# One pick signal per portion of four, and gathers in pairs behind TensorE's blocks

## The reference, cut to what matters

```python
# 32 tables; ids: [1024, 32]; 64 numbers for each field of each row
e = jnp.stack([tbl_f[ids[:, f]] for f in range(32)], axis=1)        # [1024, 32, 64]
p, q = e[:, ROW_IDX], e[:, COL_IDX]                                 # the 496 pairs i < j
z = jnp.einsum('bne,hne,bnh->bn', p, kernel, q)                     # [1024, 496]
h = jnp.concatenate([z, dense_ctx], axis=1)                         # 496 + 16 = 512
h = jnp.maximum(h @ W_top1 + b_top1, 0.0)                           # 512
h = jnp.maximum(h @ W_top2 + b_top2, 0.0)                           # 256
y = h @ W_top3                                                      # [1024, 1]
```

## Time and profile before

| | |
|---|---|
| median of 3 runs | 469.64 us (468.99 to 469.80) |
| the profiled execution, its own time | 470.17 us |
| its span, first to last instruction | 468.4 us |
| PE busy (matmuls) | 412.4 us, 88% |
| DVE busy | 353.3 us, 75% |
| ACT busy | 337.2 us, 72% |
| POOL busy | 242.3 us, 52% |
| mean granted TensorE clock | 0.967 |

### The profile page before, as it was taken

The page is one execution under the profiler, slowest core; times in us unless marked ns, Lnnn a source line. Parts: engine busy times, 40 slices in busy tenths (PEclk is TensorE's granted clock), DMA queues, the critical chain, the costliest instruction groups (busy, mean ns, idle before and its releaser), DMA issues.

```text
span 468.4 us, 13663 instructions
## 1 busy us (share of the span) xinstructions
PE 412.4 (88%) x4890; PEld 307.4 (66%) x4890; DVE 353.3 (75%) x449; ACT 337.2 (72%) x2889; POOL 242.3 (52%) x260
## 2 busy tenths in 40 slices
PE   6655779788989998999989998999989998999997
PEld 6544565667757775767757765767757775667775
DVE  0236767577887978887887978887887978889982
ACT  1125856549887797949797788949797797949992
POOL 5555554555655555565555555565555555552000
PEclk9779879799999999999999999999999999999999
DMA  3456550001111011111111010111111010010000
GB/s 73 152 194 198 187 165 21 18 18 23 24 22 23 20 25 21 24 21 22 21 22 22 20 25 18 23 23 23 23 22 23 20 24 22 22 21 13 2 4 0
DMA packets 14563, 19.27 MB, mean 41 GB/s; under 512 B 7192, under 2 KB 7840, under 8 KB 14496
## 3 DMA queue, kind: packets, MB, share of 16 engines
q0 software_dynamic: 8192, 8.40, 8.3%
q1 hardware_dynamic: 6304, 10.00, 6.6%
HBM read 18.39 MB, written 0.00 MB: 39 GB/s over the span
## 4 chain that ended last, share of the span: by engine, by line
PE 54%; DVE 27%; issue 10%; another core or an unknown queue 5%; DMA 2%; POOL 1%; ACT 0%; DVEq 0%
PE u_ps L633 23%; PE u_ps L626 16%; DVE prod_t L525 12%; DVE prod_s L542 11%; PE side_ps L647 7%; DVE h L556 4%; PE side_ps L682 2%; PE u_ps L609 2%; POOL emb L388 1%; DMA emb<-tbl,ids_sb 1%; PE acc_ps L682 1%; PE side_ps L706 1%; PE u_ps L713 1%; DVE emb_t L514 0%
## 5 line engine op out<-in xcount | busy, mean ns | idle before, releaser
L437 ACT ACTIVATE prod_s<-prod_s 128x64 f32<-128x64 f32 x1405 | 310.9, 297 | 86.6 <-DVE prod_s L542 65.0
L388 POOL DMA_INDIRECT emb<-tbl,ids_sb x256 | 242.1, 946 | 184.2 <-issue 44.0
L437 ACT ACTIVATION_READ_ACCUMULATOR prod_s<-prod_s 128x1 f32 x1405 | 268.8, 225 | 3.3 <-issue 3.2
L525 DVE TENSOR_TENSOR prod_t<-u_ps,emb_t 128x1024 f32<-128x1024 f32 x128 | 154.7, 1219 | 61.9 <-remote 26.0
L626 PEld LDWEIGHTS u_ps<-emb_t,k_sb 64*128 64x128 f32 x2048 | 141.4, 194 | 53.5 <-issue 25.8
L626 PE MATMUL u_ps<-emb_t,k_sb 64*128 64x128 f32 x2048 | 154.1, 286 | 23.3 <-DVE prod_t L525 9.5
L542 DVE TENSOR_TENSOR prod_s<-u_ps,emb 128x1024 f32<-128x1024 f32 (+4 forms) x224 | 150.4, 719 | 21.2 <-PE u_ps L633 11.5
L633 PE MATMUL u_ps<-k_sb,emb_t 64*128 64x512 f32 (+5 forms) x704 | 144.0, 496 | 17.3 <-DVE prod_s L542 10.3
L633 PEld LDWEIGHTS u_ps<-k_sb,emb_t 64*128 64x128 f32 x704 | 62.0, 194 | 48.6 <-DVE prod_s L542 18.5
L647 PE MATMUL side_ps<-prod_t,pick_sb 128*32 128x256 f32 x1024 | 64.2, 382 | 0.2 <-issue 0.2
L682 PE MATMUL acc_ps<-h_t,w_sb 64*128 64x128 f32 x336 | 47.4, 278 | 0.5
(11 more groups left out here) (32 smaller groups left out, 50.9 us busy)
## 6 DMA issues: line engine op xcount, KB each, us to landing
k_sb<-k_pairs SPq DMA_DIRECT2D x9, 512.0 KB, 3.8
emb<-tbl,ids_sb POOLq DMA_INDIRECT x256
k_sb<-k_pairs SPq DMA_DIRECT2D x6, 480.0 KB, 4.4
w_sb<-w SPq DMA_DIRECT2D x1, 1024.0 KB
w_sb<-w SPq DMA_DIRECT2D x1, 512.0 KB
k_sb<-k_pairs SPq DMA_DIRECT2D x1, 448.0 KB
h<-dense SPq DMA_DIRECT2D x8, 8.0 KB
out<-y_row SPq DMA_DIRECT2D x8, 0.5 KB
```

Source lines behind the costliest of these rows:

```text
L388: nc.gpsimd.indirect_dma_start(emb[t % EMBS][:, f * EMBED:(f + 1) * EMBED], None, tables[f], bass.IndirectOffsetOnAxis(ap=ids_sb[:, t, f:f ...
L437: done = nc.scalar.activation(slot, slot, ACT.Copy, accum_out=to[:, column:column + 1])
L525: done = nc.vector.tensor_tensor(prod_t[at % TRING][:].rearrange("p (h x) -> p h x", h=HALVES), u, low.unsqueeze(1).to_broadcast([P, HALVE ...
```

## The change

Only the last matmul of a portion of four picks still counts `picked` up: 4 times per tile instead of 16. The waits of ACT go by portions. The list entries that named single picks are replaced by blocks, so that pairs of gathers wait for one block. In `GATHER_AT` (with gather numbers): 13 from pick 0 and 14 from pick 3 to block 23; 17 from pick 4 and 18 from pick 7 to block 27; 22 from pick 10 to block 31 (where 21 waits already). In `OWN_GATHER_AT`: 26 from pick 15 of the tile before to block 4. In `SECOND_GATHERS`: 15 from pick 1 to block 25, and 18 from pick 5 to block 27.

```diff
 GATHER_AT = [
     ("u", 9), ("u", 10), ("u", 12), ("mlp", 2), ("u", 13), ("u", 14), ("u", 15), ("u", 17), ("u", 18), ("mlp", 4),
-    ("u", 19), ("u", 21), ("u", 22), ("pick", 0), ("pick", 3), ("u", 24), ("u", 26), ("pick", 4), ("pick", 7),
-    ("u", 28), ("u", 29), ("u", 31), ("pick", 10)]
+    ("u", 19), ("u", 21), ("u", 22), ("u", 23), ("u", 23), ("u", 24), ("u", 26), ("u", 27), ("u", 27), ("u", 28),
+    ("u", 29), ("u", 31), ("u", 31)]
 OWN_GATHER_AT = [
-    ("u", 0), ("u", 1), ("u", 3), ("pick", 15), ("u", 4), ("u", 5), ("u", 6), ("u", 8), ("mlp", 0)]
+    ("u", 0), ("u", 1), ("u", 3), ("u", 4), ("u", 4), ("u", 5), ("u", 6), ("u", 8), ("mlp", 0)]
...
 SECOND_GATHERS = [
     ("u", 12), ("u", 13), ("u", 14), ("u", 15), ("turn", 5), ("u", 16), ("u", 17), ("u", 18), ("u", 19), ("u", 20),
-    ("turn", 6), ("u", 21), ("u", 22), ("u", 24), ("u", 25), ("pick", 1), ("u", 26), ("u", 27), ("pick", 5),
+    ("turn", 6), ("u", 21), ("u", 22), ("u", 24), ("u", 25), ("u", 25), ("u", 26), ("u", 27), ("u", 27),
     ("u", 28), ("u", 29), ("u", 30), ("u", 31)]
...
-PORTION = NT // 4
+PORTIONS = 4
+PORTION = NT // PORTIONS
...
-                        if kind == "pick":
-                            pool.wait_ge(picked, at + 1)
-                        else:
-                            pool.wait_ge(slot_emptied, SLOT_USE[kind, 0, at] + 1)
+                        pool.wait_ge(slot_emptied, SLOT_USE[kind, 0, at] + 1)
...
-                        elif kind == "pick":
-                            of = tile - 1 if at >= 3 * PORTION else tile
-                            pool.wait_ge(picked, of * NT + at + 1)
...
-                    act.wait_ge(picked, (t + 1) * NT + PORTION)
+                    act.wait_ge(picked, (t + 1) * PORTIONS + 1)
...
-            act.wait_ge(picked, TILES * NT)
+            act.wait_ge(picked, TILES * PORTIONS)
...
                                 start=(b == 0), stop=(b == NT - 1))
+                if stop % PORTION == 0:
                     done.then_inc(picked, 1)
```

## The result

The changed kernel is slower: 476.61 us, median of 4 runs (476.51 to 476.70), against 469.72 for the kernel before on the same chip (4 runs, 468.99 to 469.98). The ratio is 1.0155 (95% interval 1.0139 to 1.0170), or +6.9 us. The forecast was 465.6 with a range from 459.5 to 475.

What follows compares the result with a forecast made beforehand. It took POOL's gathers holding PE's signals, together with PE, as the bound; 6 x (-1.2 - 0.2 + 0.15) + 7 x 0.5 = -4.0 us gave 465.6 against the median of 469.64, range 459.5 to 475.

Steps and rivals of the forecast that it cites:

- The reading: PE's signals are held while POOL processes gathers, about 1.48 us per gather in a train (a run without a pause).
- I take 1.2: Gather 22 to block 31: DVE's 1.75 us stall before block 2 shrinks, gaining 1.2 us per tile in six tiles.
- nothing changes: Rival: each gather holds as long as before and waits only move; within 0.9 us of 469.6; chance 0.17.
- I take -0.2 per tile: Gathers 17 and 18 to block 27: block 29 reaches DVE at 249.6 instead of 249.80, -0.2 us per tile.
- +0.15 for 13 and 14: Gathers 13 and 14 to block 23: PE's block 27 needs block 24's slot, costing 0.15 us per tile.
- cover gone: Worse case for 13 and 14: DVE's idle 0.52 and 0.54 no longer covers late block 24, costing 0.5 us.
- -0.69 to +0.6: Bounds for 17 and 18 per tile: all of PE's early-turn stop comes back, or the late copy shifts everything.
- some 26 records behind a held signal: Where PE was read to stop before the change: at the early turn (0.27 and 0.42 us) and third block (0.70).
- Gather 26: Moved to block 4: a train of three delays DVE's copy of transposed part 1, +0.5 us in each of seven tiles.
- The late spread takes it back: Rival: the train from gather 25 delays transposed part 1 by 1.8 us per tile, about 474.6 us; slower case's chance 0.25.
- All comes back: Rival: block 2 slips through and PE never stops at the early turn, -12.6 us, about 458; chance 0.14.
- Signals by their number: Rival: signals cost by number alone, so 96 fewer give back 0 to 4.8 us, middle 467.2; chance 0.04.

Runs made afterwards that it cites:

- e3: Kernel before with gathers 17 and 18 waiting for block 27 instead of picks 4 and 7, all 16 signals kept: 475.22 us, ratio 1.0145.
- e11: Kernel before with gather 10 waiting for block 20 instead of block 19, nothing else: 467.84 us, ratio 0.9966.
- e10: Kernel before with gather 17 alone moved to block 27, 18 staying on pick 7: 469.56 us, ratio 1.0005.
- e4: Kernel before with gather 22 waiting for block 31 instead of pick 10, all 16 signals kept: 468.74 us, ratio 0.9991.
- e9: Kernel before, 16 signals, with gathers 13 and 14 moved to block 23 and 17 and 18 to block 27 together: 474.07 us, ratio 1.0091.
- e2: Kernel before with gathers 13 and 14 waiting for block 23 instead of picks 0 and 3, all 16 signals kept: 472.16 us, ratio 1.0055.
- e5: Changed kernel, all gathers placed as there, but with all 16 pick signals per tile: 476.00 us, ratio 1.0151.
- e6: Kernel before with signals only at the six picks something waits for; tile 1's gathers 15 and 18 on blocks 25 and 27: 468.73 us, ratio 0.9999.
- e8: Kernel before without the gathers of tiles 2 to 7 and PE's waits for them, all 16 signals kept: 419.68 us, ratio 0.8950.

## Why the prediction was wrong

**The reading held.** A hold of about 1.48 us per gather, in trains, gave the right instant of each new wait in the profile after, within 0.5 us (four starts of DVE, above), and the semaphore changes show it for trains of one to four. e3 (a pair becomes three: slower) and e11 (a three becomes two: faster) agree in sign; e10, where hardly a gather moves, costs nothing. What failed is what a wait is worth.

**The step that failed most is "I take 1.2" for gather 22.** It put down 6 x 1.2 = -7.2 us and e4 measured -0.6. I took DVE's 1.75 us in the chain for time of the tile. DVE is busy for 43.9 of 52.5 us and catches up. And 0.83 of the wait only moved, to block 0: a hold over block 0 by the new pair is not in the prediction, though its own times for the pair (251.1 and 252.3) give one, to 251.1 + 3.0 = 254.1. That much of "the waits only move", which the rival "nothing changes" says, came true. Had I asked what PE does meanwhile, I would have found one stop of 0.70, the most that I could have expected back there, and in e4 it became one of 0.81.

**The second is "I take -0.2 per tile" for gathers 17 and 18, with +0.15 for 13 and 14.** Together -0.3 us; e9 measured +4.6. For 13 and 14 the prediction gave 0.5 per tile "cover gone", and 0.47 is what e2 shows: it took block 24 as done in time and only its signal as late, but PE itself stops 0.57 inside block 24, and the 0.52 and 0.54 of DVE idle that I named as cover don't cover a stop of PE. For 17 and 18 I counted a gain from gather 19 and kept only -0.69 to +0.6. The premise was that the slips belong to the signals per pick; e5 and e6 show that PE stops with 4, 6 and 16 of them, so the 0.69 was never theirs to give back, and with the longer train the stop grew to 1.15, which the prediction had at zero. Nor did its count of "some 26 records behind a held signal" carry over: after the change PE stops 10 and 15 records behind the last signal of a portion.

**Gather 26 was priced right**: 7 x 0.5 = +3.5 predicted, +2.9 alone and +3.0 to +3.4 in the changed kernel. The three errors add up: 6.6 for gather 22, 4.9 for 13 to 18 and -0.6 for 26 are the 10.9 between -4.0 and +6.9.

**The rivals.** "The late spread takes it back" gave 474.6, close to the time measured, by another way. It needed 1.8 us per tile at part 1, and got 0.4 to 0.5, though DVE does wait 2.00 there. It would have won only because the gain that it had to outweigh was missing. "Nothing changes" is out as a time. "All comes back" is out with block 2 released in time and the time unmoved. "Signals by their number" is out with e6: at 26.3 ns each, the figure of the Trainium skill's page "TensorE: Matmul & The Clock Gate" (The cost: per-tile semaphore tail), 80 signals would be an estimated 2.1 us or 0.45%, outside the interval of e6 (to 0.13% at most). In this kernel, with one such increment behind every eight records, no run shows that price.

**What stays open.** In the 30 us behind block 23 of this tile PE's stops of over 0.15 are 2.2 us after the change (0.57, 1.15, 0.16, 0.29) where they were 1.4 (0.27, 0.42, 0.70). That is 0.8 us, as much as this tile became longer; in the rest of the tile somewhat shorter stops and 0.3 us more of busy time cancel. The other steady tiles lost 0.6 to 1.5 us, and I haven't read them one by one. That the gathers hold PE's signals is shown; by which way they do it (POOL's work on them or their transfers), and why PE's own stream stops at the same times, no run here separates. Nor does one say how much of the 49 us of e8 is the holding.

## What to carry to other kernels

A wait of an engine that is not the bound is worth only what it takes from the bound: before pricing a stall of DVE in the chain, look at what PE does just behind it, since here 1.8 us of idle were worth 0.1 per tile and 2.0 were worth 0.5; and ask which signal a moved gather will hold next. When gathers on POOL hold up signals, their grouping counts, here by 2.5 us or more for one gather that made a pair a train of three (e3), and 1.6 the other way (e11): keep them to pairs with a step of the consumer that comes true after the release, and don't let several wait for one block. Price a move by its position in its train, and try the same reading in the direction that shortens a train; it found a faster kernel here.

## What the runs showed of the hardware

PE's signals are held while indirect gathers are in work, about 1.4, 3.0, 4.4 and 5.9 us from the start of a train of one, two, three and four, while DVE's go on. PE's own stream stops at such times too, for up to 1.16 us at the early turn (e9); the two large stops after the change end at 242.99 and 249.92, within 0.25 us of the ends of holds at 243.2 and 250.0.

Leaving out 192 gathers, and PE's waits for them, saved 49 us of 469, 0.26 us for each gather, about half of it in busy time of PE: the turned blocks of two steady tiles took 37.6 us with gathers and 34.0 without, for the same 512 matmuls. The mean length of a record is nearly the same (279 and 275 ns), so the records start further apart (PE by line, before, then e8).

```profile
L626 PE MATMUL u_ps<-emb_t,k_sb 64*128 64x128 f32 x512 | 37.6, 279 | 2.5 <-issue 1.5 <-DVE prod_s L542 0.6 <-DVE prod_t L525 0.4
```

```profile
L624 PE MATMUL u_ps<-emb_t,k_sb 64*128 64x128 f32 x512 | 34.0, 275 | 0.0
```

Stops of PE close together (0.46 and 1.00 us in one tile of e3, 0.48, 0.41 and 0.17 in another) were followed by about three microseconds at the half clock, up to 1.7 us lost each time; a single stop of 1.16 (e9) or 1.44 (before) was not.
